# Layer-0 attention on one NeuronCore: the first slot of each head, with the next query product ahead of the turn, and turned rows ahead of the rope at group borders

## The reference, cut to what matters

```python
H, KV, D = 16, 4, 128            # 16 query heads, 4 key/value heads (groups)
xqkv = x @ Wqkv                  # x: 1024 x 256, modulated layer norm of the input
xq, xk, xv = split(xqkv)
xq, xk = rope(xq), rope(xk)      # x1*cos - x2*sin, x1*sin + x2*cos
xk, xv = repeat(xk, 4), repeat(xv, 4)
scores = q @ k.T * D ** -0.5
probs = softmax(scores + causal_mask)
att = probs @ v
out = att @ Wo                   # summed over the 16 heads, then gated and added to x
```

## Time and profile before

| what | value |
|---|---|
| median of 3 runs | 771.89 us |
| the profiled execution's own time | 772.87 us |
| its span (first to last instruction) | 771.1 us |
| layer-0 attention's slots in the span | 32 to 433 us |
| TensorE (PE) busy | 718.0 us, 93% |
| VectorE (DVE) busy | 549.7 us, 71% |
| ScalarE (ACT) busy | 443.2 us, 57% |
| GpSimd (POOL) busy | 381.1 us, 49% |
| mean granted TensorE clock | 0.994 of full speed |

### The profile page before, as it was taken

One profiled execution on the slowest core, in us unless ns is written; L12 is line 12 of the kernel. 1 busy time (PEld: TensorE's weight loads), 2 busy tenths in 40 slices (PEclk: granted clock), 3 DMA queues, 4 the chain that ended last, 5 costly groups with the idle time before them and its releaser, 6 DMA issues. The chain is left out here.

```text
span 771.1 us, 12344 instructions
## 1 busy us (share of the span) xinstructions
PE 718.0 (93%) x4376; PEld 618.8 (80%) x4376; DVE 549.7 (71%) x1228; ACT 443.2 (57%) x914; POOL 381.1 (49%) x411
## 2 busy tenths in 40 slices
PE   7979989999999999999998799999879999799997
PEld 4858878888888888888887699997768778577787
DVE  4567786667766787767776688776578788557666
ACT  2666666667666675667656333323578776545432
POOL 3786556645766357652351330003756545215773
PEclk8999999999999999999999999999999999999999
DMA  7000000000000000005000040004000000000001
GB/s 252 14 8 8 8 22 15 14 8 8 22 15 8 8 15 14 14 8 172 7 8 8 1 137 1 1 1 134 32 0 1 1 1 2 0 4 0 1 1 56
DMA packets 19115, 19.85 MB, mean 26 GB/s; under 512 B 2158, under 2 KB 17006, under 8 KB 19054
## 3 DMA queue, kind: packets, MB, share of 16 engines
q1 hardware_dynamic: 17934, 18.40, 7.4%
q10 hardware_dynamic: 1120, 0.66, 0.3%
HBM read 18.01 MB, written 1.05 MB: 25 GB/s over the span
## 5 line engine op out<-in xcount | busy, mean ns | idle before, releaser
L611 ACT ACTIVATE at_probs<-at_probs,at_negmax 128x128 f32<-128x128 f32 (+7 forms) x128 | 99.6, 778 | 31.9 <-DVE at_negmax L711 30.0
L910 POOL TENSOR_TENSOR at_swapped<-at_swapped,at_sin 128x512 f32<-128x512 f32 x40 | 52.0, 1300 | 132.3 <-ACT at_swapped L589 132.3
L711 DVE CUSTOM_DVE_ANT_0 at_probs<-at_scores,causal 128x128 f32<-128x128 f32 (+7 forms) x128 | 96.1, 751 | 16.9 <-PE at_scores L59 16.1
L502 PE MATMUL at_turn<-ident_sb,at_probs 128*128 128x128 f32 x576 | 85.0, 274 | 13.2 <-DVE at_full_T_lo L727 11.0
L502 PEld LDWEIGHTS at_turn<-ident_sb,at_probs 128*128 128x128 f32 x576 | 66.5, 141 | 21.8 <-issue 8.4
L604 ACT ACTIVATE at_edge_T_hi<-at_turn 128x128 fp32r<-128x128 f32 (+3 forms) x128 | 55.5, 434 | 33.0 <-PE at_turn L502 32.6
L57 PE MATMUL at_scores<-at_kT_hi,room 128*128 128x512 f32 (+1 forms) x192 | 66.3, 346 | 3.4 <-DVE at_negmax L711 3.4
L604 ACT ACTIVATE at_full_T_hi<-at_turn 128x512 fp32r<-128x512 f32 x64 | 38.3, 598 | 49.6 <-PE at_turn L502 47.3
L58 PE MATMUL at_scores<-at_kT_lo,room 128*128 128x512 f32 (+1 forms) x192 | 66.6, 347 | 0.0
L59 PE MATMUL at_scores<-at_kT_hi,room 128*128 128x512 f32 (+1 forms) x192 | 66.4, 346 | 0.0
L727 DVE TENSOR_TENSOR at_edge_T_lo<-at_turn,at_edge_T_hi 128x128 fp32r<-128x128 f32 (+3 forms) x128 | 61.3, 479 | 1.2 <-ACT at_edge_T_hi L604 0.9
(11 more groups left out here) (393 smaller groups left out, 2295.0 us busy)
## 6 DMA issues: line engine op xcount, KB each, us to landing
at_wq_in<-L_attn_Wqkv SPq DMA_DIRECT2D x16, 128.0 KB, 2.2
at_wo_in<-L_attn_Wo SPq DMA_DIRECT2D x16, 128.0 KB, 2.0
staging<-L_ffn_routed_w SPq DMA_DIRECT2D x7, 256.0 KB, 4.6
ff_wmod<-L_wmod SPq DMA_DIRECT2D x1, 1536.0 KB, 6.6
at_wmod<-L_wmod SPq DMA_DIRECT2D x1, 1024.0 KB, 9.6
staging<-L_ffn_w_gate SPq DMA_DIRECT2D x1, 1024.0 KB, 5.4
staging<-L_ffn_w_up SPq DMA_DIRECT2D x1, 1024.0 KB, 7.5
staging<-L_ffn_w_down SPq DMA_DIRECT2D x1, 1024.0 KB, 9.9
```

Of the source, the lines that this page charges most:

```text
L502: mm = pe.transpose(p_turn[t % 2][:, b - b0, :], probs[:, s % 4, b * P:(b + 1) * P], m.ident[:, :])
L611: act.activation(row, row, ACT.Exp, scale=-1.0, bias=negmax[:, unit % 4:unit % 4 + 1], accum_out=rowsum[:, unit // NT % 2, i:i + 1])\
L711: dve.tensor_tensor_reduce(out=probs[:, s % 4, 0:width], in0=p_scores[s % 2][:, 0:width], in1=m.causal[:, S - width:], scale=-1.0, scalar= ...
L910: turning = pool.tensor_tensor(swapped[:, r % 2, :], swapped[:, r % 2, :], sin[:, cols], ALU.mult)
```

## The change

TensorE: in the first slot of heads 1, 2 and 3 of each group, except head 15 (11 heads), the query product is issued ahead of the turn, after a wait for the exponentials of that turn's unit, which the turn waits for too. Group borders keep TensorE's order. ScalarE and VectorE: at the three group borders the turned rows (and on VectorE the maximum) are treated ahead of the rope's first steps; elsewhere their order stays.

```diff
@@ TensorE, slot
                     scores(g, h, i)
                     if unit < 4:
                         value_job(4 + unit)
+                    query_first = i == 0 and h > 0 and query_here(g, h, i)
+                    if query_first:
+                        pe.wait_ge(exp_done, unit - 1)
+                        query_job(head + 1, 0, query_bank(0))
                     if unit >= 2:
                         turn(unit - 2)
                     if i in (2, 3) and head:
                         attend(head - 1, 1, 4 * (i - 2), 4 * (i - 1))
                     if i == 6:
                         attend(head, 0, 0, 4)
-                    if query_here(g, h, i) and not (i == 0 and h == 0 and g):
+                    if query_here(g, h, i) and not query_first and not (i == 0 and h == 0 and g):
@@ ScalarE, slot
+                    if unit >= 2:
+                        probs_hi(unit - 2)
                     if i == 0 and h == 0 and g:
                         copy_rope(rope_number["query", head + 1, i], query_bank(i))
-                    if unit >= 2:
-                        probs_hi(unit - 2)
                     exp(unit)
@@ VectorE, slot
-                    if i == 0 and h == 0 and g:
-                        cos_rope(rope_number["query", head + 1, i], 0, query_bank(0), query_free)
                     maximum(unit)
                     if i == 2 and head:
                         inverse_sums(head - 1)
                     if unit >= 2:
                         probs_lo(unit - 2)
+                    if i == 0 and h == 0 and g:
+                        cos_rope(rope_number["query", head + 1, i], 0, query_bank(0), query_free)
```

## The result

The changed kernel takes 776.67 us (median of 4 runs, 775.43 to 777.7) against 771.92 of the kernel before: ratio 1.0059, 95% interval 1.0043 to 1.0074, slower. A second measurement, beside the last experiments, gave 775.8 us and 1.0054 (1.0041 to 1.0066). The prediction was 774.7, slower by 0.36%; direction and mechanism came out, the loss is larger than its sum.

A forecast was written before the change was run, and what follows sets the result against it. The prediction took TensorE to bound the kernel. Eleven heads at +4.0 us and three borders at -1.2 made +2.8, from the median 771.89 to 774.7 us; the range was 771.8 to 777.1.

The forecast's parts named there:

- the loop of 0.64 + 0.63 + 0.83 us: Turn to high part, to low part, to the turn reusing its bank: second turn at least 2.10 us after the first.
- The pause of 0.52: TensorE's idle time before slot 0's turn in ordinary heads: 0.52 us gained by filling it, about 0.95 lost in slot 1.
- Borders: At three group borders, turned rows ahead of the rope win about 0.39 us each, not 0.69; 1.2 us in all.
- The short wait forecast before the values product: At group borders, a new wait of about 0.3 us before the values product of slot 2.
- Part 1: Eleven heads with the query product ahead of the turn in their first slot: +4.0 us in all, slower.
- later by 0.43: Slot 1 of heads 2, 5, 6, 9, 10: bank free for tile 7's turn at 262.35 instead of 261.92; 2.15 us in all.
- holds where a key product follows and TensorE reaches the values product of slot 2 late enough: Condition under which the 0.43 us delay was taken as each head's whole loss: heads 2, 5, 6, 9 and 10.
- Rule and row: Query product costed at the trace's 1.40 us (0.233 a matmul); the skill's 216 ns rule gives 1.29, sum near +1.7.
- The pause is filled, and nothing waits in its place: Rival: slot 1 does not wait, heads win 6.8 us and borders 1.2, giving 763.9 us; chance 0.08.
- The borders win all they can: Rival: borders gain 0.69 each or up to 4.9 in all, or part 1's delay is absorbed; 771.0 to 773.8; chance 0.17.
- The delays spread: Rival: borders win nothing and every head loses 0.5 to 0.55 us, +5.2, giving 777.1 us; chance 0.12.
- It doesn't do what it says: Rival: tile 6's exponentials come late, so the pause before slot 0's turn stays; +7.5 us, 779; chance 0.03.

The follow-up runs named there:

- two matmuls ahead: The changed kernel with only two of the query product's six matmuls ahead of the turn, four behind it: 766.51 us, 0.9939 of the kernel before.
- The parts measured apart: Against the kernel before: only TensorE's new order in eleven heads, 776.74 us, 1.0066; only the new ScalarE and VectorE order at three borders, 770.25 us, 0.9986.

## Why the prediction was right, and where it was short

- **Bound and loop: right.** TensorE is the bound, and the loop of 0.64 + 0.63 + 0.83 us is the limit of the second turn: 2.11 us measured in the changed kernel, 2.14 with two matmuls ahead. The pause of 0.52 was filled, and 0.98 appeared in slot 1 (0.82 shown and 0.16 of modelled ends) for a forecast 0.95.
- **Borders: right in size and reason.** 0.39 each, held by the values product and the order on ScalarE; alone they make 0.9986. The short wait forecast before the values product shows in its weight load (0.32).
- **Part 1: right in sign, +4.0 forecast and +5.0 by the offsets.** Two terms of the sum were too small.
  - In every one of the eleven heads 0.06 to 0.09 was missing, about 0.7 us in all. The query product took 1.44 us behind the short scores matmuls, not the 1.40 of the earlier trace rows, and a few hundredths came at other steps. This is the whole difference in heads 1, 3, 7, 11, 13 and 14.
  - The other 0.3 us are in "later by 0.43" for the five heads with a key product, which measured 0.56: 0.50 up to tile 2, and 0.06 more at the output product of slot 5. The step behind it, that it "holds where a key product follows and TensorE reaches the values product of slot 2 late enough", looked for slack at one place only. It is there, but slot 5 has none: the chain from the rope copy through GpSimd passes on the copy's delay of 0.55, where TensorE's own is 0.50. A third rope buffer takes these 0.06 away. GpSimd's sum of idle time says nothing on that.
- **Rule and row.** The section's 216 ns for 512 columns (the Trainium skill, TensorE: Matmul & The Clock Gate, Back-to-back issue gap), which it gives for a single isolated matmul, would have made the sum +1.7. The rows have 0.233 and more for each, and the measurement decides for them.
- **Rivals.** "The pause is filled, and nothing waits in its place": the wait in slot 1 excludes it. "The borders win all they can": no, 0.39; nor did head 2 absorb the delay, it lost 0.58. "The delays spread" (777.1) was the nearest in number, and half of it came: the heads do lose about 0.55 each, but the borders won. "It doesn't do what it says": the product starts at 261.08, right behind the scores.
- **Where the total lies.** The measured 4.75 us between the medians is 0.9 more than the offsets' 3.9, and 776.67 lies close to the upper end of the range, 777.1. The parts measured apart give 1.0052, 4.0 us, and the repeat 1.0054, so that remainder is within what the intervals allow.

## What to carry to other kernels

Work that fills a pause pays only up to the length of the pause; what is longer delays the instruction behind it. If that instruction starts a loop over other engines, the same work is missing where it hid the loop. Cut the filler to the pause (here two matmuls of six, 0.35 us won a head in place of 0.55 lost). And look for slack at every place where another chain meets the bound engine, not only at the next one. A place where the filler is missing anyway, as in head 15 here, shows the loop's price beforehand.

## What the runs showed that was not expected

- A wait can bind with no idle time in the profile: the changed kernel's output product at 278.18 starts 0.05 us after the addition that it needs, inside the modelled end of the turn. A delay of 0.55 in that chain came through in full.
- The name of a releaser can be wrong: the wait in slot 1 is laid to the exponentials in ordinary heads and to the low part at borders, where the exponentials end later. It is the same wait of 0.82.
- A third rope buffer wins 3.4 us alone (0.9955). The first head wins 4.7 by the offsets, where GpSimd's backlog from the start holds ScalarE for 4.5 us, and the next one gives part of it back.
